# Scattering the last row's expert lists between the gathers of the first expert blocks, in a decoder layer on one core

## The chip, the cores and the metric

The kernel runs on one core of a Trainium2 chip. The metric is the device time of one execution in microseconds; lower is better. Engines: PE (TensorE), DVE (VectorE), ACT (ScalarE), POOL (GpSimd) and SP (SyncE, which only issues DMAs here).

## The reference

One decoder layer over x (4 rows of 512 tokens, 512 wide): attention, then a state-space scan that takes a context, then a mixture of experts. The change lies in the start of the last of these:

```python
logits = x @ gate_weight.T                      # 2048 tokens, 32 experts
topv, topi = top_k(softmax(logits), 8)
active = scaled >= 0.05                         # at least the best one stays
for e in experts:                               # w_gu: 512 -> 384, w_d: 192 -> 512
    g, u = split(x @ w_gu[e].T)
    acc = acc + (silu(g) * u) @ w_d[e].T * combine[:, e]
return x + acc
```

## The kernel before

The four rows pass through attention and scan one after the other. At the end of each row DVE works out, for each of its 512 tokens, the routing weights (`entry`, 33 numbers: 32 weights and the token's number) and up to eight places (`slot[:, t, k]`), one in the list of each expert that the token is active for. MAX8 puts them in the order of the experts: place k = 0 belongs to the token's lowest expert, so the list of expert e is filled by the scatters of k = 0 to e and by none of a higher k. POOL writes the lists into DRAM by indirect DMAs (`send`, line 2039), one for each t (4 tiles of 128 tokens) and k (8): 32 scatters a row. Those of the first three rows count on one semaphore, `sent`; those of the last row on eight, `sent0` to `sent7`, one for each k (`send_last`).

After the last row DVE counts the lists and writes a table of blocks (`tab`, `blocks`, lines 1947 to 1974; `rows_ok` says it is there). A block is 128 entries of one expert's list; each expert has at least two (`MIN_BLK`), and here there are 68 in all. A quad is four blocks. Each block passes through these steps:

- SP (`load_quad`) loads the block's weights (`meta`, line 469) and its token numbers (`get_ids`, line 470), and the numbers once more for the add (`add_ids`, line 473). For the first 16 blocks (`early`), block b first waits until `sent` of k = b // 2 has landed.
- POOL gathers the 128 token rows (`get`, line 2072) into one of four buffers `x_blk`, once `get_ids` is there (`get_in`) and PE has transposed the buffer's last block (`xt_ps`). `get_next(q, r)` gathers the block that lies six behind q * 4 + r.
- PE transposes the block (line 519), ACT and DVE split it in a high and a low part (`xt_hi`, line 1396; `xt_lo`, line 1979), PE multiplies by the expert's gate and up weights (lines 917 to 919), ACT and DVE make the hidden activations, PE transposes them and multiplies by the down weights (lines 932 to 936), and ACT weighs the result into one of four `y_ring` buffers (line 1409).
- POOL adds the block into `out` by an indirect DMA that accumulates (`add`, line 2078). `add_pair` waits for y, for `add_ids`, and for earlier adds to have landed.

PE's order is written out by hand: gate_up of block b + 1, the transposes of block b + 3, down of block b, the transposes of b + 1's hidden activations. So a gather that is late holds up the down product of the block three ahead of it. POOL executes its DMAs in the order of the program; so does SP. The expert weights are loaded by ACT's queue, four experts ahead.

The lines of SP that make a block wait for its scatters, and POOL's order before the change:

```python
if early and r % MIN_BLK == 0:
    sp.wait_ge(S[f"sent{(q * QUAD + r) // MIN_BLK}"], TT * 16)
```

```
k0 k1 k2 k3 k4 | gathers 0 1 2 3 | gathers 4 5 | k5 gathers 6 7 adds 0 1 | k6 gathers 8 9 adds 2 3 | k7 gathers 10 11 adds 4 5 | gathers 12 13 adds 6 7 | ...
```

Of the kernel before, what the change touches and what calls it, by code (L numbers as in the profile page):

```python
# [35 lines left out]
NE, INTER, TOPK, TAU = 32, 192, 8, 0.05  # L36
# [5 lines left out]
QUAD = 4  # L42
# [97 lines left out]
def decoder_layer(nc, a):  # L140
    ctx = ExitStack()
    with ctx:
# [38 lines left out]
        def sb(name, shape, dt=F32):  # L181
# [74 lines left out]
        r = {n: o_t[:].rearrange("p h t -> p (h t)")[:, 12 * T + i * TT * NE:12 * T + (i + 1) * TT * NE].rearrange("p (t e) -> p t e", t=TT)  # L256
             for i, n in enumerate(NAMES)}
# [52 lines left out]
        def wait_apart(eng, semaphore, value):  # L310


            if isinstance(value, int):
                eng.wait_ge(semaphore, value)
                return
            count = eng.to_reg(value)
            eng.wait_ge(S["w_in_sb"], 16 * N_W)
            eng.wait_ge(semaphore, count)
# [1710 lines left out]
        def _(pool):  # L2029
# [7 lines left out]
            def send(t, k, sent):  # L2037

                pool.indirect_dma_start(out=lists, out_offset=bass.IndirectOffsetOnAxis(ap=slot[:, t, k:k + 1].bitcast(U32), axis=0),  # L2039
                                        in_=entry[:, t, :], in_offset=None, bounds_check=LIST_ROWS - 1, oob_is_err=False).then_inc(sent, 16)  # L2040
# [23 lines left out]
            def send_last(ks):  # L2064

                for k in ks:
                    for t in range(TT):
                        send(t, k, S[f"sent{k}"])

            def get(r):  # L2070

                pool.indirect_dma_start(out=x_blk[:, r, :], out_offset=None, in_=xf_dram,
                                        in_offset=bass.IndirectOffsetOnAxis(ap=get_ids[:, r:r + 1].bitcast(U32), axis=0),
                                        bounds_check=NTOK - 1, oob_is_err=False).then_inc(S[f"blk_in{r}"], 16)

            def add(r):

                pool.indirect_dma_start(out=out, out_offset=bass.IndirectOffsetOnAxis(ap=add_ids[:, r:r + 1].bitcast(U32), axis=0),  # L2078
                                        in_=y_ring[:, r, :], in_offset=None, compute_op=ALU.add).then_inc(S[f"added{r % 2}"], 16)

            def get_next(q, r):

                far = r + QUAD + 2
                fq, fr = far // QUAD, far % QUAD
                wait_apart(pool, S[f"get_in{fr}"], q * 32 + (fq * 32 + 32))
                wait_apart(pool, S["xt_ps"], q * QUAD + (far - QUAD + 1))
                get(fr)

            def landed_before(q, r):
                return pool.value_load(blocks[0:1, bass.ds(q * QUAD + (B_LANDED + r), 1)], min_val=ADDED0 - 16, max_val=ADDED0 + MAX_BLK * 8)  # L2090

            def add_pair(q, r):

                landed = [landed_before(q, r), landed_before(q, r + 1)]
                for i in range(2):
                    wait_apart(pool, S[f"add_in{r + i}"], q * 16 + 16)
                for i in range(2):
                    wait_apart(pool, S["yb_ok"], q * QUAD + (r + i + 1))
                    wait_apart(pool, S[f"added{i}"], q * 32 + (ADDED0 + (r // 2) * 16))
                    wait_apart(pool, S[f"added{1 - i}"], landed[i])  # L2100
                    add(r + i)

            pool.wait_ge(S["slot_ok"], NB)

            send_last(range(0, 5))
            pool.wait_ge(S["xf_out"], NB * 16)
            pool.wait_ge(S["blank_ok"], 1)
            pool.wait_ge(S["rows_ok"], 2)
            for r in range(QUAD):
                pool.wait_ge(S[f"get_in{r}"], 32)  # L2110
                get(r)
            last_quad = pool.value_load(tab[0:1, T_LAST:T_LAST + 1], min_val=NE * MIN_BLK // QUAD - 1, max_val=MAX_BLK // QUAD - 1)
            pool.wait_ge(S["x2_out"], NB * 16)
            for r in range(2):
                get_next(-1, r + 2)
            for q in range(2):
                for r in range(0, QUAD, 2):
                    k = q * 2 + r // 2 + 5
                    if k < TOPK:
                        send_last(range(k, k + 1))  # L2120
                    get_next(q, r)
                    get_next(q, r + 1)
                    add_pair(q, r)
            with pool.Fori(2, last_quad) as q:
                for r in range(0, QUAD, 2):
                    get_next(q, r)
                    get_next(q, r + 1)
                    add_pair(q, r)
# [47 lines left out]
```

## Time and profile before

| | us |
|---|---|
| median of three runs | 1611.66 |
| lowest, highest | 1605.77, 1620.83 |
| the profiled execution | 1605.77 |
| its span, first to last instruction | 1604.0 |
| last row's scatters begin | 1228.78 |
| first gather of the expert phase | 1254.52 |
| mean granted TensorE clock | 0.947 of full speed |

All times in the rows are microseconds from the start of the profiled execution's span. The span ends with the expert phase, so what this phase starts later or loses is in the time in full, unless a later stretch has slack. A timeline's row gives the start, the duration, the engine, the line, what is written and read, and in brackets how long the engine had been idle and what ended that. SPq is SP's own queue; the row of a DMA there is its issue. The chain of waits follows the end of the program back to its start, from each instruction to what released it.

### The profile page before, as it was taken

The page shows a single profiled execution, that of the slowest core. Times are in us where ns is not written, and L with a number is a line of the kernel's source. Part 1 is how long each engine was busy: PE and PEld are TensorE (multiplying, and loading weights), DVE is VectorE, ACT ScalarE, POOL GpSimd, SP SyncE. Part 2 cuts the span into 40 slices and gives each one's busy share as a digit, 9 for nine tenths or more (in the row PEclk, how much of TensorE's full clock was granted, in tenths as well). Part 3 has the DMA queues.
Part 4 walks back from the last instruction along what each step waited for, and adds up shares of the span by engine and source line. Part 5 has one row for each costly group of instructions (what it writes and reads, how often), then busy time and mean ns, then how long its engine had stood idle before and what let it go on. Part 6 is the DMA issues. An engine that isn't in the chain of part 4 may idle for free.

```text
span 1604.0 us, 25043 instructions
## 1 busy us (share of the span) xinstructions
PE 1391.2 (87%) x6762; PEld 993.4 (62%) x6763; DVE 1222.9 (76%) x1459; ACT 972.1 (61%) x2484; POOL 472.7 (29%) x307
## 2 busy tenths in 40 slices
PE   4799889999999899989999998998943489999996
PEld 1577666547777554667765366776422367777775
DVE  4477768959898996889899688899986156776763
ACT  6677665477876546787654578866420246666663
POOL 0000000000000781000068300004842576655663
PEclk9799999999999999999999899999975689999998
DMA  6693333222253221235313232520701379999994
GB/s 241 239 287 101 90 105 93 66 65 83 78 171 106 87 76 42 93 92 158 93 61 116 55 92 80 142 69 29 239 32 39 66 167 239 252 240 245 244 212 64
DMA packets 128788, 202.45 MB, mean 126 GB/s; under 512 B 44984, under 2 KB 46473, under 8 KB 127552
## 3 DMA queue, kind: packets, MB, share of 16 engines
q1 hardware_dynamic: 75120, 86.70, 18.7%
q0 software_dynamic: 27840, 63.83, 16.9%
q10 hardware_dynamic: 25744, 50.87, 9.9%
q8 instruction: 44, 0.72, 0.2%
q14 instruction: 40, 0.33, 0.1%
HBM read 170.57 MB, written 46.21 MB: 135 GB/s over the span
## 4 chain that ended last, share of the span: by engine, by line
PE 40%; DVE 34%; ACT 11%; issue 7%; DMA 2%; ACTq 2%; another core or an unknown queue 1%; POOL 1%; SPq 1%; DVEq 0%; POOLq 0%
DVE state L1581 12%; PE pair_o L661 6%; DVE dbu L1573 5%; DVE dbu L1587 5%; DVE y L1592 4%; PE bank L643 4%; PE bank L797 4%; PE pair_o L797 3%; PE bank L917 2%; PE pair L595 2%; PE pair L597 2%; PE pair L596 2%; ACT decay L1117 2%; PE pair L519 2%; PE bank L918 2%
## 5 line engine op out<-in xcount | busy, mean ns | idle before, releaser
L2039 POOL DMA_INDIRECT lists<-entry,slot x128 | 253.9, 1983 | 207.6 <-DVE slot L1764 169.8
L1581 DVE TENSOR_TENSOR_SCAN state<-decay,dbu 128x2048 f32<-128x2048 f32 x64 | 283.0, 4422 | 7.5 <-ACT decay L1117 4.0
L661 PE MATMUL pair_o<-v_aug,probs 128*128 128x129 f32 x2048 | 250.7, 281 | 8.9 <-ACT probs L1111 8.6
L2035 POOL DMA_DIRECT2D wq<-wq_dram x30 | 21.5, 719 | 783.6 <-PE pair L597 670.0
L661 PEld LDWEIGHTS pair_o<-v_aug,probs 128*128 128x128 f32 x2048 | 241.2, 196 | 17.7 <-ACT probs L1111 16.8
L1117 ACT ACTIVATE decay<-delta,neg_a 128x511 f32<-128x511 f32 x256 | 165.0, 738 | 100.4 <-DVE state L1581 93.7
L1111 ACT ACTIVATE probs<-bank 128x512 f32<-128x512 f32 x256 | 146.5, 606 | 88.1 <-PE bank L643 51.2
L2078 POOL DMA_INDIRECT out<-y_ring,add_ids x68 | 118.4, 1742 | 101.3 <-DMA out<-y_ring,add_ids 70.7
L1587 DVE TENSOR_TENSOR dbu<-state,c_bc 128x2048 f32<-128x2048 f32 x64 | 146.6, 2291 | 1.6
L1573 DVE TENSOR_TENSOR dbu<-du,b_bc 128x2048 f32<-128x2048 f32 x64 | 146.3, 2287 | 1.6
L1592 DVE TENSOR_TENSOR y<-y,dbu 128x2048 f32<-128x2048 f32 x60 | 137.2, 2287 | 1.1
L643 PE MATMUL bank<-q_t,k_t 128*128 128x512 f32 x256 | 122.7, 614 | 12.0 <-ACT q_t L1099 6.8
L797 PE MATMUL bank<-wout,o_t 128*128 128x512 f32 x256 | 125.0, 620 | 0.9 <-DMA wout<-in_wout 0.9
L797 PE MATMUL pair_o<-wout,o_t 128*128 128x512 f32 x256 | 120.3, 600 | 0.0
L595 PE MATMUL pair<-wq,xn_hi 128*128 128x512 f32 x256 | 106.7, 417 | 4.4 <-ACT q_s L1082 3.5
L917 PE MATMUL bank<-w_hi,xt_hi 128*128 x272 | 100.1, 368 | 8.0 <-DVE xt_lo L1979 6.9
L597 PE MATMUL pair<-wq,xn_lo 128*128 128x512 f32 x256 | 100.7, 393 | 0.0
L596 PE MATMUL pair<-wq,xn_hi 128*128 128x512 f32 x256 | 100.6, 393 | 0.0
L1632 DVE TENSOR_TENSOR w_lo<-w_raw,w_hi (+1 forms) x64 | 95.4, 1494 | 1.9
L918 PE MATMUL bank<-w_lo,xt_hi 128*128 x272 | 93.9, 345 | 0.0
L919 PE MATMUL bank<-w_hi,xt_lo 128*128 x272 | 93.8, 345 | 0.0
L1071 ACT ACTIVATE junk<-pair 128x128 bf16<-128x128 f32 x256 | 67.3, 291 | 39.0 <-PE pair L597 39.0
(239 smaller groups left out, 2690.3 us busy)
## 6 DMA issues: line engine op xcount, KB each, us to landing
wq<-wq_dram POOLq DMA_DIRECT2D x30, 1024.0 KB, 8.5
w_raw<-in_w_exp ACTq DMA_DIRECT2D x32, 768.0 KB
wout<-in_wout SPq DMA_DIRECT2D x64, 256.0 KB
b_bc<-bc_dram SPq DMA_DIRECT2D x64, 256.0 KB
c_bc<-bc_dram SPq DMA_DIRECT2D x64, 256.0 KB
w_raw<-in_w_exp ACTq DMA_DIRECT2D x32, 512.0 KB
lists<-in_const ACTq DMA_DIRECT2D x1, 8712.0 KB, 49.3
q_s<-in_x SPq DMA_DIRECT2D x4, 1024.0 KB, 5.1
```

Of the source, the lines that this page charges most:

```text
L595: pe.matmul(bank_q[t % 2][:], xn_hi[:, k, tile], wq[:, 0, k, :], start=(k == 0), stop=False)
L597: mm = pe.matmul(bank_q[t % 2][:], xn_lo[:, k, tile], wq[:, 0, k, :], start=False, stop=(k == KT - 1))
L643: mm = pe.matmul(bank_s[k % 2][:], k_t[:, tile], q_t[:, j, :], start=True, stop=True)
L661: mm = pe.matmul(bank_o[half][:, (t % 2) * (DH + 1):(t % 2 + 1) * (DH + 1)], probs[:, k, t * P:(t + 1) * P], v_aug[:, k, :], start=(k == 0 ...
L797: mm = pe.matmul((bank_o + bank_s)[t][:], o_t[:, h, t * P:(t + 1) * P], wout[:, h % 4, :], start=(h == 0), stop=(h == H - 1))
L1111: act.activation(probs[:, k, :], bank_s[k % 2][:], ACT.Exp).then_inc(S["exp_ok"], 1)
L1117: act.activation(dA3[:, e, 1:], delta[:, e, 1:], ACT.Exp, scale=neg_a[:, bass.ds(n, 1), e:e + 1].rearrange("p a c -> p (a c)")).then_inc(S ...
L1573: dve.tensor_tensor(dbu[:], du[:], b_bc[:, i:i + 1, :].to_broadcast([P, ET, T]), ALU.mult).then_inc(S["dbu_ok"], 1)
L1581: dve.tensor_tensor_scan(state[:].rearrange("p e t -> p (e t)"), dA, dbu[:].rearrange("p e t -> p (e t)"), 0.0, ALU.mult, ALU.add).then_in ...
L1587: dve.tensor_tensor(dbu[:], state[:], c_bc[:, i:i + 1, :].to_broadcast([P, ET, T]), ALU.mult).then_inc(S["bc_free"], 1)
L1592: dve.tensor_tensor(dst[:], y[:], dbu[:], ALU.add).then_inc(S["y_ok"], 1)
L2039: pool.indirect_dma_start(out=lists, out_offset=bass.IndirectOffsetOnAxis(ap=slot[:, t, k:k + 1].bitcast(U32), axis=0), in_=entry[:, t, :] ...
```

## The change

POOL issues the last row's scatters in another order. k0 and k1 stay ahead of the gathers. k2 now lies between the gathers of blocks 1 and 2, k3 behind the gather of block 3, and k4 to k7 each directly ahead of a pair of gathers (before, k5 to k7 stood ahead of pairs of gathers two slots earlier). The order is then:

```
k0 k1 | gathers 0 1 | k2 | gathers 2 3 | k3 | gathers 4 5 | gathers 6 7 adds 0 1 | k4 gathers 8 9 adds 2 3 | k5 gathers 10 11 adds 4 5 | k6 gathers 12 13 adds 6 7 | k7 gathers 14 15 adds 8 9 | ...
```

SP, PE, ACT and DVE are as before. The loads, gathers and adds are the same ones.

```diff
-            send_last(range(0, 5))
+            send_last(range(0, 2))
             pool.wait_ge(S["xf_out"], NB * 16)
             pool.wait_ge(S["blank_ok"], 1)
             pool.wait_ge(S["rows_ok"], 2)
-            for r in range(QUAD):
+            for r in range(2):
                 pool.wait_ge(S[f"get_in{r}"], 32)
                 get(r)
+            send_last(range(2, 3))
+            for r in range(2, QUAD):
+                pool.wait_ge(S[f"get_in{r}"], 32)
+                get(r)
+            send_last(range(3, 4))
+            for r in range(2):
+                get_next(-1, r + 2)
             last_quad = pool.value_load(tab[0:1, T_LAST:T_LAST + 1], min_val=NE * MIN_BLK // QUAD - 1, max_val=MAX_BLK // QUAD - 1)
             pool.wait_ge(S["x2_out"], NB * 16)
-            for r in range(2):
-                get_next(-1, r + 2)
             for q in range(2):
                 for r in range(0, QUAD, 2):
-                    k = q * 2 + r // 2 + 5
-                    if k < TOPK:
+                    k = q * 2 + r // 2 + 3
+                    if k in range(4, TOPK):
                         send_last(range(k, k + 1))
                     get_next(q, r)
                     get_next(q, r + 1)
                     add_pair(q, r)
+            send_last(range(TOPK - 1, TOPK))
             with pool.Fori(2, last_quad) as q:
```

## Rows read from the trace of the kernel before

**Rows 1.** Table of stretches: length, busy time (instructions) by engine, PEclk, DMA share, GB/s.

```profile
1206.00:1258.00 52.00, 14.04 (x73) 11.38 (x74) 23.38 (x85) 2.70 (x5) 21.72 (x22) 0.53 0.11 30
1258.00:1325.00 67.00, 51.71 (x237) 42.26 (x238) 28.25 (x57) 27.48 (x48) 42.12 (x34) 0.85 0.61 137
1325.00:1560.00 235.00, 227.16 (x1180) 182.32 (x1179) 163.04 (x307) 153.39 (x257) 144.29 (x102) 1.00 0.98 242
```

**Rows 2.** Chain of waits, 1180 to 1604 us: start, length, what it is.

```profile
1254.52 3.25 DMA x_blk<-xf_dram,get_ids
...
1272.51 8.45 another core or an unknown queue
...
1290.13 2.26 another core or an unknown queue
...
1308.97 3.37 another core or an unknown queue
```

**Rows 3.** Timeline of POOL: scatters (L2039), gathers (L2072) and adds (L2078).

```profile
1237.80 0.98 POOL L2039 DMA_INDIRECT lists<-entry,slot  x1 [0.30 <-issue]
...
1253.23 0.98 POOL L2039 DMA_INDIRECT lists<-entry,slot  x1 [0.30 <-issue]
1254.52 1.05 POOL L2072 DMA_INDIRECT x_blk<-xf_dram,get_ids  x1 [0.30 <-issue]
...
1262.98 1.00 POOL L2072 DMA_INDIRECT x_blk<-xf_dram,get_ids  x1 [5.27 <-DMA get_ids<-lists]
...
1275.81 1.05 POOL L2072 DMA_INDIRECT x_blk<-xf_dram,get_ids  x1 [0.31 <-issue]
1277.17 1.02 POOL L2072 DMA_INDIRECT x_blk<-xf_dram,get_ids  x1 [0.30 <-issue]
...
1305.67 0.98 POOL L2039 DMA_INDIRECT lists<-entry,slot  x1 [0.30 <-issue]
...
1309.64 1.63 POOL L2078 DMA_INDIRECT out<-y_ring,add_ids  x1 [0.30 <-issue]
...
1313.46 1.08 POOL L2072 DMA_INDIRECT x_blk<-xf_dram,get_ids  x1 [0.30 <-issue]
...
1323.49 1.08 POOL L2072 DMA_INDIRECT x_blk<-xf_dram,get_ids  x1 [0.30 <-issue]
```

**Rows 4.** Timeline of SP's queue: issues of the block loads.

```profile
1247.87 0.02 SPq L470 DMA_DIRECT2D get_ids<-lists  x1
...
1256.33 0.70 SPq L470 DMA_DIRECT2D get_ids<-lists  x1
...
1259.95 0.35 SPq L469 DMA_DIRECT2D meta<-lists  x1
...
1262.04 0.35 SPq L469 DMA_DIRECT2D meta<-lists  x1
...
1310.86 0.69 SPq L469 DMA_DIRECT2D meta<-lists  x1
```

**Rows 5.** Timeline of DVE: the last write of the block table.

```profile
1239.36 0.40 DVE L1974 CAST blocks<-bank 1x256 int32<-1x256 f32 x1
```

**Rows 6.** Timeline of ACT: blocks 0 and 14 taken up (xt_hi), y of block 0.

```profile
1259.05 0.60 ACT L1396 ACTIVATE xt_hi<-pair 128x512 fp32r<-128x512 f32 x1 [43.01 <-PE pair L519]
...
1271.55 0.69 ACT L1409 ACTIVATE y_ring<-pair_o,meta 128x512 f32 x1 [0.97 <-issue]
...
1336.32 0.60 ACT L1396 ACTIVATE xt_hi<-pair  x1 [0.17 <-issue]
```

**Rows 7.** Timeline of PE: one gate_up product after the 8 us gap, one later.

```profile
1282.72 0.52 PE L918 MATMUL bank<-w_lo,xt_hi 128*128 x1
...
1288.18 0.34 PE L918 MATMUL bank<-w_lo,xt_hi 128*128 x1
```

**Rows 8.** Line 2039 in 1050 to 1200 us and 1200 to 1320 us: duration ns min/median/max.

```profile
L2039 POOL DMA_INDIRECT lists<-entry,slot x32: 980/2022/4162, 1101.6 to 1182.8; - x32
...
L2039 POOL DMA_INDIRECT lists<-entry,slot x32: 980/982/1748, 1228.8 to 1305.7; - x32
```

## The prediction

> **What bounds the kernel now.** I read four views in this order. First the table of stretches: from 1325 to 1560 us PE is busy for 227.16 of 235 us at a granted clock of 1.00, so the expert phase, once it runs, is limited by TensorE and can't catch up what it lost earlier. Before it lie two poor stretches: 1206 to 1258 us (PE busy 14.04 of 52) and 1258 to 1325 us (51.71 of 67, clock 0.85) [rows 1]. These two are all that the change touches. Then the chain of waits: it enters the expert phase through the scatters of the lists, then the gather of block 0 (issued at 1254.52, landed 3.25 us later), then PE's first transposes. Behind that it names pieces of 8.45, 2.26 and 3.37 us that no recorded work explains [rows 2]. Then POOL's timeline: the eighth of the last row's 32 scatters starts at 1237.80 and the twentieth at 1253.23, a pitch of 1.286 us; the gather of block 0 waits behind all twenty [rows 3]. Last SP's queue, which loads the token ids that each gather needs [rows 4].
>
> **The change part by part.** No instruction is added or removed. What moves is where POOL issues scatters. Before: k0 to k4, gathers 0 to 5, then k5, k6 and k7 each ahead of a pair of gathers. After: k0, k1, gathers 0 and 1, k2, gathers 2 and 3, k3, gathers 4 to 7, adds 0 and 1, then k4, k5, k6 and k7, each directly ahead of its own pair of gathers and adds. The wait for x2_out moves too, behind gathers 4 and 5. SP issues that store ahead of xf's, and xf_out is waited for ahead of gather 0 already, so I cost it at nothing; were x2 late, add 0 and gather 6 would wait, in both kernels.
>
> What matters is a wait that isn't in the diff: SP loads the ids of blocks 2k and 2k+1 only when the scatters of slot k have landed (the early part of load_quad). Before, k5 stood ahead of the gathers of blocks 6 and 7, which need k3: two slots of slack. After, k4 stands ahead of blocks 8 and 9, which need k4 itself: no slack, four times over.
>
> *The head start.* The blocks' table is ready at 1239.36 + 0.40 = 1239.76 [rows 5]; eight scatters end at 1237.80 + 1.29 = 1239.09, so neither waits for the other. Then SP must load the ids of block 0. From a load of meta to the gather is 1262.98 - 1259.95 = 3.03 us [rows 3, 4]. At the earliest gather 0 starts at 1239.76 + 3.03 = 1242.8. At the latest SP is as slow as before, get_ids at 1247.87, and the gather 3.03 later, 1250.9. Nothing says which, so I take the middle, 1246.9. That is 7.6 us ahead of 1254.52.
>
> *POOL's order from there.* SP's pitch from one block to the next is 1262.04 - 1259.95 = 2.09 us [rows 4]; a gather takes 1277.17 - 1275.81 = 1.36 of POOL, two adds 1313.46 - 1309.64 = 3.82, four scatters 4 x 1.286 = 5.14 [rows 3]. Gather 1 at 1249.0, k2 from 1250.4 to 1255.5, gathers 2 and 3 to 1258.2, k3 with its last scatter at 1262.1 and over at 1263.4, gathers 4 and 5 to 1266.1. Gather 6 must wait for the ids that depend on k3.
>
> *The price of that wait,* W, from the start of the last scatter of a slot to the gather of its first block. Upper end: the last scatter of k7 starts at 1305.67 and SP's load of meta for block 14 at 1310.86, 5.19 us, though that load also waited for a free buffer; plus 3.03 for meta to gather, 8.2. Lower end: the scatter's own 0.98 and the 3.03, 4.0, with a landing that costs nothing more. No row shows the landing alone; I take the middle, W = 6.1.
>
> The Trainium skill bears on this (DMA: Bandwidth & Descriptors, section Anatomy of one DMA, SWDGE path): it gives a DMA issued by GpSimd a fixed cost of about 2.0 us whatever its size, most of it the receipt of the last write before the semaphore moves. By that page W would be about 2.0 + 3.0, some 5 us, which is the point from which the first rival decides, and the sum below would be about 0; the 3.25 us of the gather above, which also moves data, doesn't contradict it.
>
> So gather 6 is at 1262.1 + 6.1 = 1268.2, gather 7 at 1270.3, add 0 at 1271.6; y of block 0 is ready by then (17.0 us after its gather, as 1271.55 - 1254.52 [rows 3, 6], is 1263.9). Adds end at 1275.5. From here each slot costs POOL three scatter pitches 3.86 + W 6.1 + 2.09 for the second gather + 1.36 + 3.82 = 17.2 us. Gather 14 comes after k4, k5, k6 and then k7: 1275.5 + 3 x 17.2 + 3.86 + 6.1 = 1337.1, against 1323.49 before.
>
> *What of it is on the path.* Before, ACT takes up block 14 at 1336.32, and gather 0 was picked up 1259.05 - 1254.52 = 4.53 us after its issue [rows 3, 6]; so gather 14 was needed only by 1331.8. After, it is 5.3 us late, PE has waited for it, and behind it there are 54 blocks at PE's own pace. POOL catches up at once (two gathers and two adds are 6.5 us a pair), so the lateness stays 5.3 and doesn't grow. Waiting also lowers PE's clock: a gate_up matmul takes 0.52 us after the 8 us gap and 0.34 later [rows 7]; twelve of them are 2.2 us, and I add one such block. Sum: 5.3 + 2.2 = +7.5 us. The profiled execution took 1605.77 us, which is the fastest of three with a median of 1611.66; the sum gives 1613.3 against the first and 1619.2 against the median, which is what I predict.
>
> **The rivals.**
>
> *The head start stays.* If W is near its lower end (4.0), the slot costs 15.1 us and gather 14 is at 1337.1 - 5 x 2.1 = 1326.6 (k3's W and four more), before 1331.8. It is 5.2 us early, and PE, which started 7.6 earlier, keeps that much: 1611.7 - 5.2 = 1606.5. With gather 0 at 1242.8 rather than 1246.9 PE keeps the 7.6: 1604. It decides at W = 5.0, where 5 x 1.1 takes the whole lateness away. For it: before, gather 14 is issued 8.3 us ahead of its need (1331.8 - 1323.49), so POOL wasn't what PE waited for. Against: no row of a scatter shows its data landed as soon as issued.
>
> *PE's unexplained pieces come with the scatters.* The 8.45, 2.26 and 3.37 us of the chain begin at 1272.51, 1290.13 and 1308.97 [rows 2]: the first just ahead of gather 6 at 1275.81, where POOL issues k5, the last 3.3 us behind k7's last scatter at 1305.67, and three scatter batches run beside PE. After the change six batches do. Three more at the mean of 4.7 are 14.1 us; if they delay y and with it POOL's adds, they come on top: 1619.2 + 14.1 = 1633.3. Against it: when PE waits for POOL anyway, such a piece is hidden, and POOL's pauses between scatters and gathers may even end them.
>
> *SP stays slow.* Its get_ids for block 0 is at 1247.87 and for block 1 at 1256.33, 8.5 us instead of 2.09, while POOL scatters [rows 4]. If that comes back in only two of the slots, 2 x 6.4 = 12.8 us more: 1632.
>
> *Scatters take longer beside VectorE.* In the stretch of VectorE's long scans 32 scatters had a median of 2022 ns, up to 4162; in the last batch it is 982, up to 1748 [rows 8]. If the 16 scatters of k4 to k7 cost 1.04 us more each, that is 16.6: 1636. The Trainium skill has the reason (SBUF, State Buffer, section Who interferes with whom: a VectorE instruction in a two-port mode holds the port pair that it shares with GpSimd, and GpSimd is blocked until it ends). The trace shows slow scatters in the scans' stretch only, and doesn't show by itself that the port is why.
>
> **How the numbers follow.** Forecast 0.50, with its own range 1611 (no lateness is left) to 1630 (W at 8.2, 5 x 2.1 = 10.5 more); head start 0.15; pieces with the scatters 0.15; slow SP 0.13; slow scatters 0.05. The range of all, 1604 to 1636, reaches from the first rival to the last and leaves the lateness of an SP slow in all slots outside. A measurement of this kernel tells about 1% from no change, 16 us, so faster means below 1595.5 and slower above 1627.8. Even the head start alone doesn't reach the first: 0.05 for faster, for a W at its end together with pieces that vanish. Slower takes nearly all of the last three rivals, less where they overlap with hidden waits: 0.29. Within 1%: 0.66.
>
> **What would show it.** Right: gather 0 at about 1247, PE's first transposes about 7 us earlier; POOL idle for 3 to 5 us between each of k4 to k7 and the gather behind it, ended by get_ids; gather 14 at about 1337; PE waiting for x_blk in 1280 to 1340; from 1345 the same pace as before. Wrong: POOL not idle behind the scatters (head start), more pieces of unexplained time while x_blk has landed (second rival), SP's loads 8 us apart (third), scatters over 2 us (fourth). The forecast falls altogether if gather 14 starts before 1331.8 and the time still rises.

## The result: 2.6% slower, and half of it is lost after the change's own stretch

| | us |
|---|---|
| after, median of 4 (lowest, highest) | 1654.3 (1649.44, 1667.81) |
| before, median of 4 in the same comparison | 1612.55 (1605.77, 1620.83) |
| ratio, 95% interval | 1.0257 [1.0211, 1.0304] |
| the profiled execution's span | 1652.1, before 1604.0 |
| mean granted TensorE clock in it | 0.929, before 0.947 |

The prediction was 1619.2 us, within 1604 to 1636. The kernel is outside of it, on the slow side. All ratios in this document compare fast executions alone, while the medians have the slow ones in them too (here the one of 1667.81 us, in e10 two of twelve, and in one comparison a single 4568.49 us of the kernel before).

To compare traces I count from T0, the start of the first of the last row's 32 scatters. T0 itself isn't the change's: it lies behind the same instructions in all kernels, and over all profiles here it is at 1221.9 to 1240.0 us. In the two main profiles it is 1228.8 (before) and 1237.7 (after), so 9.0 of the 48.1 us between the spans lie ahead of anything that was changed. The other 39.1 us are the subject. Each number of this table is one row's time less T0:

| us after T0 | before | after | later by |
|---|---|---|---|
| gather of block 0 | 25.7 | 15.1 | -10.6 |
| add of block 0 | 49.7 | 40.4 | -9.3 |
| gather of block 14 | 94.7 | 120.1 | 25.4 |
| y of block 14 | 123.2 | 143.2 | 20.0 |
| y of block 67, the last | 364.7 | 398.9 | 34.2 |
| end | 375.2 | 414.4 | 39.1 |

20.0 us are lost up to y of block 14, and another 14.2 between there and the last block, where the two programs are the same. The remaining 4.9 fall in the tail behind it. These are the numbers of one profiled execution each; the last experiments give second and third profiles.

The table of stretches of after, with the columns of [rows 1] (length, then busy time and instructions of PE, PEld, DVE, ACT, POOL, then PEclk, DMA share, GB/s):

```profile
1206.00:1258.00 52.00, 17.75 (x76) 14.70 (x76) 28.84 (x99) 3.91 (x10) 11.55 (x12) 0.50 0.17 55
1258.00:1325.00 67.00, 45.50 (x214) 37.30 (x215) 25.52 (x52) 25.00 (x45) 36.74 (x32) 0.82 0.46 110
1325.00:1560.00 235.00, 197.79 (x987) 154.91 (x986) 138.61 (x258) 127.85 (x214) 144.45 (x95) 0.95 0.85 207
```

The stretches are counted from the start of the span, in which T0 of after lies 9.0 us later. Against [rows 1], PE is busy 3.7 us more in the first stretch (the head start), 6.2 less in the second, and 29.4 less in the third, which the prediction took to be PE's own.

POOL's timeline of after shows the head start and the waits behind the late scatters:

```profile
1246.74 0.98 POOL L2039 DMA_INDIRECT lists<-entry,slot  x1 [0.30 <-issue]
1252.83 1.04 POOL L2072 DMA_INDIRECT x_blk<-xf_dram,get_ids  x1 [5.11 <-DMA get_ids<-lists]
...
1309.82 1.90 POOL L2039 DMA_INDIRECT lists<-entry,slot  x1 [0.30 <-issue]
1316.63 1.05 POOL L2072 DMA_INDIRECT x_blk<-xf_dram,get_ids  x1 [4.91 <-DMA get_ids<-lists]
1319.26 1.01 POOL L2072 DMA_INDIRECT x_blk<-xf_dram,get_ids  x1 [1.58 <-DMA get_ids<-lists]
1321.11 1.63 POOL L2078 DMA_INDIRECT out<-y_ring,add_ids  x1 [0.83 <-DMA add_ids<-lists]
1323.04 1.58 POOL L2078 DMA_INDIRECT out<-y_ring,add_ids  x1 [0.31 <-issue]
1324.92 1.04 POOL L2039 DMA_INDIRECT lists<-entry,slot  x1 [0.30 <-issue]
...
1349.77 0.98 POOL L2039 DMA_INDIRECT lists<-entry,slot  x1 [0.30 <-issue]
1357.85 1.05 POOL L2072 DMA_INDIRECT x_blk<-xf_dram,get_ids  x1 [7.09 <-issue]
```

and SP's queue beside it, the loads that follow the last scatters of slots k5 and k7:

```profile
1313.69 0.35 SPq L469 DMA_DIRECT2D meta<-lists  x1
...
1354.76 0.35 SPq L469 DMA_DIRECT2D meta<-lists  x1
```

Gather 0 is at 1252.83 instead of 1254.52 although T0 is 9.0 us later. Then each slot stands still: from the last scatter of k5 (1309.82) SP takes 3.87 us to its next load and 2.94 more to the gather; behind k7 (1349.77) it is 4.99 and 3.09. The row at 1357.85 is the gather of block 14. What PE did meanwhile is in the waits of 1258 to 1400 us (engine and line, what it waited for, total us, times, longest):

```profile
PE pair L519 <- DMA x_blk<-xf_dram,get_ids: 43.0, 8, 10.7
...
POOL x_blk L2072 <- DMA get_ids<-lists: 22.5, 5, 7.4
```

PE waits 43.0 us for gathered blocks. That is the predicted mechanism, and it is larger than predicted. The second loss is in the waits of 1400 to 1560 us, past all scatters. Before:

```profile
POOL out L2078 <- DMA out<-y_ring,add_ids: 42.8, 18, 3.2
ACT y_ring L1409 <- PE pair_o L936: 25.8, 27, 1.0
```

After:

```profile
ACT y_ring L1409 <- PE pair_o L936: 42.5, 33, 2.4
...
POOL out L2078 <- DMA out<-y_ring,add_ids: 27.8, 11, 3.7
...
PEld pair_o L932 <- issue: 9.0, 13, 1.4
...
PE pair_o L932 <- DMA out<-y_ring,add_ids: 2.0, 2, 1.1
```

In both kernels POOL's add waits for an earlier add to land, 42.8 and 27.8 us. What is new is that PE's down product (line 932), which has no row at all in this view of before, now waits as well: a y_ring buffer is free only when the add four blocks back has landed, and PE waits for that (`added`) ahead of `down`. The view puts only 2.0 us of it down to the adds by name; the 9.0 us of the weight load it calls "issue", which names no releaser. The chain of waits for the same 160 us is plainer; these are its shares by line, cut at the end. Before:

```profile
by line: issue 20.9%; PE bank L917 11.8%; PE bank L918 9.7%; PE bank L919 9.6%; PE pair L519 6.1%; ACT xt_hi L1396 4.8%; PE pair_o L936 4.1%; PE bank L519 3.8%; ACTq L1302 3.7%; PE pair_o L932 2.4%; PE pair_o L935 2.2%; DVE xt_lo L1979 2.2%
```

After:

```profile
by line: DMA out<-y_ring,add_ids 37.7%; issue 13.2%; DMA x_blk<-xf_dram,get_ids 8.1%; DMA get_ids<-lists 5.1%; PE bank L917 3.2%; DMA add_ids<-lists 3.1%; PE bank L919 2.6%; PE bank L918 2.6%; PE pair L519 2.5%; PE pair_o L936 1.9%; PE pair
```

Before, the adds aren't in the chain and PE's products are. After, the landing of adds is its largest part. The same view of the other profiles divides them in the same way: the landing of adds has 63 to 75% in e1 to e5, e8, e10 and e11, none in e9a, 6.3% in e9b (the kernel before both times), and none in e6 and e7, whose adds are shorter. Two questions follow: how much each half of the change costs, and whether the slower pace is a lasting effect of a single late gather.

### The profile page after: what moved, and what is told of

It is laid out like the page before. It is cut to its first block, busy times and chain, and to the rows that moved or that the text cites. A ratio compares the mean times of both kernels' runs of the same rounds, so it can differ in the third digit from the quotient of the medians.

```text
span 1652.1 us, 25043 instructions
## 1 busy us (share of the span) xinstructions
PE 1415.5 (86%) x6762; PEld 1009.3 (61%) x6763; DVE 1223.9 (74%) x1459; ACT 970.9 (59%) x2484; POOL 490.0 (30%) x307
## 4 chain that ended last, share of the span: by engine, by line
PE 38%; DVE 28%; DMA 11%; ACT 10%; issue 7%; SPq 2%; POOL 2%; ACTq 1%; POOLq 1%; DVEq 0%
DVE state L1581 10%; PE pair_o L661 8%; DMA out<-y_ring,add_ids 7%; PE bank L643 5%; DVE dbu L1573 5%; DVE y L1592 4%; DVE dbu L1587 4%; PE bank L797 4%; PE pair_o L797 3%; PE pair L595 2%; PE pair L597 2%; PE pair L596 2%; ACT decay L1117 2%; ACT probs L1111 2%; PE bank L519 1%
## 5 line engine op out<-in xcount | busy, mean ns | idle before, releaser
L2039 POOL DMA_INDIRECT lists<-entry,slot x128 | 254.4, 1987 | 213.1 <-DVE slot L1764 175.4
L661 PE MATMUL pair_o<-v_aug,probs 128*128 128x129 f32 x2048 | 256.9, 286 | 8.6 <-ACT probs L1111 8.3
L661 PEld LDWEIGHTS pair_o<-v_aug,probs 128*128 128x128 f32 x2048 | 247.5, 200 | 17.4 <-ACT probs L1111 16.5
L1111 ACT ACTIVATE probs<-bank 128x512 f32<-128x512 f32 x256 | 146.3, 605 | 98.5 <-PE bank L643 52.1
L2078 POOL DMA_INDIRECT out<-y_ring,add_ids x68 | 126.8, 1865 | 94.2 <-DMA out<-y_ring,add_ids 44.0
L1979 DVE TENSOR_TENSOR xt_lo<-pair,xt_hi (+1 forms) x70 | 48.3, 690 | 81.2 <-ACT xt_hi L1396 79.9
L2072 POOL DMA_INDIRECT x_blk<-xf_dram,get_ids x70 | 83.9, 1198 | 60.3 <-DMA get_ids<-lists 28.4
L1396 ACT ACTIVATE xt_hi<-pair (+1 forms) x70 | 41.9, 598 | 100.0 <-PE pair L519 97.7
L1409 ACT ACTIVATE y_ring<-pair_o,meta 128x512 f32 x68 | 46.8, 688 | 85.1 <-PE pair_o L936 85.1
```

Source lines behind the costliest of these rows:

```text
L661: mm = pe.matmul(bank_o[half][:, (t % 2) * (DH + 1):(t % 2 + 1) * (DH + 1)], probs[:, k, t * P:(t + 1) * P], v_aug[:, k, :], start=(k == 0 ...
L1111: act.activation(probs[:, k, :], bank_s[k % 2][:], ACT.Exp).then_inc(S["exp_ok"], 1)
```

## The experiments

In all of them "pace" is the time for a pair of blocks, from ACT's y rows: (y of 34 - y of 14) / 10, then (y of 58 - y of 34) / 12. "Behind y" is the mean time from a block's y to the start of its add, even and odd blocks, over blocks 16 to 57.

| | median | g14 | y14 | end | pace | behind y |
|---|---|---|---|---|---|---|
| before | 1612.55 | 94.7 | 123.2 | 375.2 | 9.20, 9.20 | 3.9, 1.7 |
| after | 1654.3 | 120.1 | 143.2 | 414.4 | 10.13, 9.62 | 10.3, 7.8 |
| e1 early start, two slots of slack | 1618.07 | 97.5 | 123.7 | 388.0 | 9.47, 9.60 | 9.5, 7.0 |
| e2 early start, one slot | 1619.41 | 92.0 | 118.5 | 379.7 | 9.55, 9.38 | 9.2, 6.8 |
| e3 late half alone | 1646.6 | 120.1 | 143.4 | 413.5 | 10.15, 9.46 | 10.1, 7.6 |
| e4 after, adds first | 1638.76 | 121.4 | 144.3 | 407.0 | 9.47, 9.56 | 9.3, 6.9 |
| e5 before, one hold-up | 1620.37 | 107.5 | 129.1 | 390.6 | 9.44, 9.49 | 9.3, 6.9 |
| e6 after, half-width adds | 1628.34 | 119.7 | 141.6 | 391.1 | 9.20, 9.19 | 7.5, 5.2 |
| e7 before, half-width adds | 1592.55 | 90.1 | 116.8 | 366.7 | 9.20, 9.20 | 2.2, 1.6 |
| e8 before, only k7 late | 1616.88 | 97.6 | 122.2 | 390.3 | 10.07, 9.49 | 10.0, 7.5 |

g14 (gather of block 14), y14 and end are us after T0 in the one profiled execution; the median is over several. They differ: where a reading rests on the one or the other, the text says which. One profile is a coarse measure of the end: two profiles of one program differ there by 10.0 us (e2 and e10, see below) and by 25.0 (after and e11). The kernel before has medians of 1612 to 1615 in the comparisons, so a ratio is given for each.

**The two halves of the change.** e1 keeps the early start (k0 and k1 ahead of the first gathers) and gives k5 to k7 the two slots of slack that they had before. The cuts of e1, e3, e4 and e10 are against after, those of e5, e7 and e8 against before:

```diff
             for r in range(2):
                 get_next(-1, r + 2)
+            send_last(range(4, 5))
...
-                    k = q * 2 + r // 2 + 3
-                    if k in range(4, TOPK):
+                    k = q * 2 + r // 2 + 5
+                    if k in range(5, TOPK):
                         send_last(range(k, k + 1))
...
-            send_last(range(TOPK - 1, TOPK))
```

> The early half of the change alone: k0 and k1, gathers 0 and 1, k2, gathers 2 and 3, k3, gathers 4 and 5, k4, then k5, k6 and k7 ahead of pairs of gathers as before, each two slots ahead of the blocks that need it. Theory A (the four waits without slack cost the time): no gather behind gather 6 waits for its ids, POOL's slots take 12 to 17 us as before, and the earlier start gives 3 to 10 us: 1603 to 1610. Rival (the early interleaving itself costs, for instance because scatters slow PE's start): slower than before, 1618 or more.

e2 is the same with one slot of slack: `k = q * 2 + r // 2 + 4` in the loop, k4 in its first round, and nothing behind it.

> The early half, with one slot of slack: k4 ahead of gathers 6 and 7, k5 ahead of 8 and 9, and so on to k7 ahead of 12 and 13. Theory A: a slot of POOL without a wait is 12 to 14 us and the scatters' landing and the ids together take 8, so one slot hides it whole: within 3 us of the kernel with two slots, 1603 to 1612. Rival (each slot taken away costs in proportion): half way to the changed kernel, about 1630.

e3 keeps only the late half: k0 to k3 ahead of all gathers, and k4 to k7 each directly ahead of its own blocks, as in after.

```diff
-            send_last(range(0, 2))
+            send_last(range(0, 4))
...
-            for r in range(2):
-                pool.wait_ge(S[f"get_in{r}"], 32)
-                get(r)
-            send_last(range(2, 3))
-            for r in range(2, QUAD):
+            for r in range(QUAD):
                 pool.wait_ge(S[f"get_in{r}"], 32)
                 get(r)
-            send_last(range(3, 4))
```

> The late half alone: k0 to k3, then gathers 0 to 7 and adds 0 and 1, then k4 to k7 each directly ahead of its own gathers as in the changed kernel. Theory A: four waits of 7 to 8 us stay, slots of 20 to 21 us, so the time is that of the changed kernel within 6 us, 1648 to 1660. Rival (early interleaving costs): near the kernel before, 1612 to 1620.

Measured: e1 1618.07 us, ratio 1.0015 [0.9972, 1.0058]; e2 1619.41, 1.0033 [0.9976, 1.0090]; e3 1646.6, 1.0189 [1.0152, 1.0226]. The late half alone costs 31.7 us (against a median of 1614.9 for the kernel before in that comparison), of the change's 41.7, and its gather 14 and y of block 14 are where those of after are (120.1 and 143.4). The early start alone brings nothing that the times can tell: e1 is at the time of its rival and not in the 1603 to 1610 expected, e2 between its two theories, and e3 1.4 us below its range. In its profiles it is real at first: gather 0 is at 15.1 instead of 25.7, and in e2 y of block 14 comes 4.7 us earlier than before. By the end that is gone, and both end later than before does from T0. Two things in the profiles stand against it. The first is a kind of wait that [rows 2] show too. The waits of e1 from 1250 to 1345 us have

```profile
ACT silu_g L1401 <- remote: 16.8, 2, 15.1
ACT xt_hi L1396 <- remote: 4.1, 3, 2.8
```

where the same view of before has

```profile
ACT silu_g L1401 <- remote: 10.7, 2, 8.5
```

"remote" means that no recorded work explains the wait. ACT waits for a PE product whose record ended long ago. The second is the pace behind block 14: 9.4 to 9.6 us a pair instead of 9.20, with gathers that were in time. So the pace isn't tied to a late gather 14, and I tested it by itself.

**One suspected cost alone.** e8 is the kernel before with k7 alone moved to directly ahead of its blocks:

```diff
-                    if k < TOPK:
+                    if k < TOPK - 1:
                         send_last(range(k, k + 1))
...
+            send_last(range(TOPK - 1, TOPK))
             with pool.Fori(2, last_quad) as q:
```

> The kernel before with k7 alone moved, from ahead of gathers 10 and 11 to directly ahead of gathers 14 and 15: one slot without slack. POOL waits 7 to 8 us once. Theory X: gather 14 had 8.3 us in hand, nothing is lost, 1609 to 1615. Theory L: the adds are late by the wait less the 2 to 4 us that they have in hand, 4 to 6 us lost, 1616 to 1619.

Measured: 1616.88 us (median of ten), 1.0033 [0.9997, 1.0069]. The wait is there, in POOL's timeline of e8:

```profile
1319.52 0.98 POOL L2039 DMA_INDIRECT lists<-entry,slot  x1 [0.30 <-issue]
1326.44 1.76 POOL L2072 DMA_INDIRECT x_blk<-xf_dram,get_ids  x1 [5.94 <-issue]
```

6.92 us for W, and gather 14 is at 97.6, inside the 103.0 by which the prediction said it was needed; y of block 14 comes at 122.2, 1.0 us ahead of before. It is late all the same. PE's timeline of e8 has, at the transposes of block 14:

```profile
1330.73 1.09 PE L519 MATMUL pair<-const,x_blk 128*128 128x128 f32 x4 [4.82 <-DMA x_blk<-xf_dram,get_ids]
```

The 103.0 comes from a profile in which PE was held back by the unexplained pieces of [rows 2]. e5 to e8 have none. In e5, which is the kernel before up to its hold-up, y of block 10 is at 98.6, and in e7 at 98.5, against 104.8 in the profile of before; in e8 it is at 95.0. From y of block 10 to y of block 12 e8 then takes 16.7 us, where before takes 9.4. So a gather is needed by a moment that moves with PE, and y14 of e5 and e8 is better held against the 116.8 of e7 than against 123.2. The larger part of the loss comes behind it: from T0 to the end the profile is 15.1 us longer than that of before (390.3 against 375.2), and from y of block 14 to the end it takes 268.1 us against 252.0, at a pace of 10.07 and then 9.49. In this execution, a POOL that was held up for 7 us never got back to where it was. The medians tell a smaller loss, 4.8 us, whose interval reaches no loss at all.

**A hold-up without any scatter.** e5 leaves the scatters where they were before and puts eight memsets of a spare tile on POOL, one after the other, ahead of the loop:

```diff
+            for i in range(8):
+                pool.memset(spare[:], 0.0).then_inc(S["idle"], 1)
+                pool.wait_ge(S["idle"], i + 1)
             with pool.Fori(2, last_quad) as q:
```

> The kernel before with POOL held up once, by eight memsets of an unused tile of 128x2048 directly ahead of gather 14, D us in all (some 15 to 25). The scatters keep their order. Theory X (only a late gather costs, and POOL catches up): gather 14 had 8.3 us in hand, so D - 8 us are lost and the pace of a pair of blocks behind it is 9.2 us as before. Theory L (POOL's adds wait for the last pair to land, so that POOL's own cycle is as long as PE's and it never catches up): D - 4 or more are lost, adds follow y by 8 to 10 us instead of 2 to 4 to the end, and the pace behind is 9.5 us or more.

Measured: 1620.37 us (median of ten, 1615.05 to 1632.32), 1.0054 [1.0034, 1.0074]. The profile shown is of its slowest execution. The spare tile and the semaphore `idle` are declared elsewhere. POOL's timeline:

```profile
1329.80 1.58 POOL L2079 DMA_INDIRECT out<-y_ring,add_ids  x1 [0.31 <-issue]
1330.82 15.45 POOL L2126 MEMSET spare<- 128x2048 f32 x8
1347.46 1.09 POOL L2073 DMA_INDIRECT x_blk<-xf_dram,get_ids  x1 [1.20 <-issue]
...
1378.49 1.63 POOL L2079 DMA_INDIRECT out<-y_ring,add_ids  x1 [1.03 <-issue]
1380.42 2.90 POOL L2079 DMA_INDIRECT out<-y_ring,add_ids  x1 [0.31 <-issue]
...
1387.54 1.63 POOL L2079 DMA_INDIRECT out<-y_ring,add_ids  x1 [0.97 <-DMA out<-y_ring,add_ids]
1389.47 2.97 POOL L2079 DMA_INDIRECT out<-y_ring,add_ids  x1 [0.31 <-issue]
...
1396.86 1.63 POOL L2079 DMA_INDIRECT out<-y_ring,add_ids  x1 [1.23 <-DMA out<-y_ring,add_ids]
```

The memsets put gather 14 12.8 us later than before; y of block 14 is 5.9 late, and the end 15.4. (Against e7, the nearer measure up to block 14, gather 14 is 17.4 late and y of block 14 12.3 late.) The even add of one pair starts at 1378.49, the next at 1387.54 and 1396.86, 9.05 and 9.32 apart, and each waits for the last pair's odd add: 1396.86 - 1389.47 = 7.39 us from the start of one to the start of the other. Over blocks 15 to 57 these are 7.53 on average, and 1.93 from the even to the odd add of a pair. That is a cycle of 9.46 us on average, longer than the 9.20 in which PE delivers a pair. The chain of e5 for 1400 to 1560 us:

```profile
by line: DMA out<-y_ring,add_ids 71.7%; issue 17.6%; POOL out L2079 6.4%; POOLq L319 1.3%; DMA get_ids<-lists 1.2%; POOLq L317 0.5%; POOLq L2128 0.5%; POOLq L318 0.4%; SPq L470 0.3%; SPq L466 0.3%; POOLq L2073 0.3%; SPq L474 0.3%; SPq L471 
```

So the expert phase can run at two paces. At the pace of before, PE sets it and the adds follow y by 3.9 and 1.7 us. At the other, the adds follow by 9.3 and 6.9 us, and the chain of adds sets it. One hold-up is enough to go from the first to the second, and behind block 14 no profile shows the way back. Ahead of it there is one: in the three profiles of before the add of block 4 is 9.8 to 9.9 us behind its y and that of block 8 only 1.7 to 3.1, while PE itself takes 11.5 to 13.8 us for a pair. The adds catch up where PE is slower than they are.

The size in the medians doesn't speak for this theory as the profile does. The memsets take 15.45 us. Theory L expected a loss of that less 4 or more, at least 11.5 us; theory X, that less 8, 7.5 us. The medians differ by 8.3.

**Shorter adds.** e6 is after and e7 is before with adds of half the width (`y_ring[:, r, 0:D // 2]` into a DRAM tensor `half` of 256 columns). Both leave out the experts' part of the output, so their times stand only against each other. Width and target change together, so which of the two shortens an add isn't separated.

```diff
-                pool.indirect_dma_start(out=out, out_offset=bass.IndirectOffsetOnAxis(ap=add_ids[:, r:r + 1].bitcast(U32), axis=0),
-                                        in_=y_ring[:, r, :], in_offset=None, compute_op=ALU.add).then_inc(S[f"added{r % 2}"], 16)
+                pool.indirect_dma_start(out=half, out_offset=bass.IndirectOffsetOnAxis(ap=add_ids[:, r:r + 1].bitcast(U32), axis=0),
+                                        in_=y_ring[:, r, 0:D // 2], in_offset=None, compute_op=ALU.add).then_inc(S[f"added{r % 2}"], 16)
```

> The changed kernel with half adds: only columns 0 to 255 of y are added, into a DRAM tensor of its own, so the experts' part of the output is left out. Against the kernel before with the same half adds. Theory L: the adds land sooner, POOL's cycle is shorter than PE's, POOL catches up and the pace is 9.2 us from about block 16; the difference to the kernel before with half adds is the slots' alone, 20 to 28 us instead of 42. Theory X: the adds have no part in it, the difference stays about 42 us.

> The kernel before with the same half adds, the experts' part of the output left out. All theories: PE is the bound, so within 6 us of the kernel before, 1600 to 1612.

Measured: e6 1628.34 us, e7 1592.55; against the kernel before 1.0083 [1.0050, 1.0115] and 0.9881 [0.9850, 0.9912]. The chain of e6 for 1400 to 1560 us:

```profile
by line: issue 21.7%; PE bank L918 9.8%; PE bank L920 7.4%; PE bank L919 7.4%; ACT xt_hi L1397 6.8%; ACTq L1303 5.5%; PE pair_o L937 4.7%; PE pair L520 4.6%; ACT silu_g L1402 3.4%; ACTq L1410 2.9%; PE pair_o L933 2.6%; PE pair_o L936 2.5%; 
```

The adds are out of the chain and PE is back in it, at a pace of 9.20 and 9.19 with the adds still 7.5 and 5.2 us behind y. The one add to the next pair's takes 7.16 + 1.97 = 9.13 us, just under PE's 9.20. From y of block 14 to that of 67 the two profiles take 241.6 and 241.3 us: the second loss has vanished, and with it nothing else, since y of block 14 is still 24.8 us late. From T0 to the end they differ by 24.4, the two profiled executions by 28.5, of which 4.0 is T0 (1239.8 and 1235.8). The medians differ by 35.8, which lies between what the two theories gave, and only 5.9 below the 41.7 of the full adds. By the ratios it is 32.6 against 41.4, with intervals that overlap. The pace is settled by the profiles, the size in the medians isn't. e7 missed its own range too: it was expected at 1600 to 1612, since PE bounds it, and is 19.6 us below the kernel before. In its profile PE's pace is the same 9.20, and from T0 to the end it is 8.5 us shorter, 6.4 of that up to y of block 14; the rest of the 19.6 is open.

**Can the wait lie beside the adds?** e4 is after with `add_pair(q, r)` ahead of the two `get_next` of each slot, so that POOL adds while SP waits for the scatters.

```diff
                         send_last(range(k, k + 1))
+                    add_pair(q, r)
                     get_next(q, r)
                     get_next(q, r + 1)
-                    add_pair(q, r)
```

> The changed kernel with one difference: in the four unrolled slots the two adds stand between the scatters and the gathers, so POOL has 3.8 us of work while the ids come. Theory A: each of three or four slots is 3.8 us shorter (about 17 us), and the time falls by 11 to 15 us from 1654, to about 1640. Rival (the length of the slots isn't what counts): unchanged at 1650 to 1658.

Measured: 1638.76 us, 1.0138 [1.0096, 1.0179], so the median is 15.5 us below that of after. The trace doesn't bear out the reason. Gather 14 is at 121.4, no earlier than in after, and POOL's timeline has

```profile
1321.65 0.98 POOL L2039 DMA_INDIRECT lists<-entry,slot  x1 [0.30 <-issue]
1333.44 1.59 POOL L2078 DMA_INDIRECT out<-y_ring,add_ids  x1 [10.81 <-issue]
1335.33 1.58 POOL L2078 DMA_INDIRECT out<-y_ring,add_ids  x1 [0.30 <-issue]
1337.21 1.08 POOL L2072 DMA_INDIRECT x_blk<-xf_dram,get_ids  x1 [0.30 <-issue]
```

The adds don't use the wait, they have it themselves: SP loads `add_ids` of a block behind `get_ids` of the block six further on, which it must not load before the scatters have landed. SP's queue in e4 shows it:

```profile
1325.05 0.33 SPq L470 DMA_DIRECT2D get_ids<-lists  x1
1326.15 0.33 SPq L473 DMA_DIRECT2D add_ids<-lists  x1
...
1328.96 0.33 SPq L473 DMA_DIRECT2D add_ids<-lists  x1
```

From T0 to the end e4 is 7.4 us shorter than after, 6.6 of it by the pace from block 14 to 34 (9.47 instead of 10.13), which is less than two profiles of one kernel differ by. I had the right time for the wrong reason, and why e4 is faster stays open.

**Can the adds be kept close?** e10 was written as e2 with another order in the slots, the adds ahead of the next scatters and gathers:

```diff
+            send_last(range(4, 5))
+            get_next(0, 0)
+            get_next(0, 1)
+            for s in range(4):
+                add_pair(s // 2, s % 2 * 2)
+                if s < 3:
+                    send_last(range(s + 5, s + 6))
+                    get_next((s + 1) // 2, (s + 1) % 2 * 2)
+                    get_next((s + 1) // 2, (s + 1) % 2 * 2 + 1)
```

> An attempt to beat both: the early start and one slot of slack, and in the unrolled slots the adds ahead of the scatters and gathers, so that adds stay close behind y. Order: k0 k1, gathers 0 1, k2, gathers 2 3, k3, gathers 4 5, k4, gathers 6 7, adds 0 1, k5, gathers 8 9, adds 2 3, k6, gathers 10 11, adds 4 5, k7, gathers 12 13, adds 6 7, then the loop. Theory L: adds 2 to 5 us behind y, pace 9.2, and 3 to 8 us faster than before, 1604 to 1609. Rival: the order of adds in the first slots doesn't last, adds 7 to 9 us behind y and 1612 to 1619 as for the kernel with one slot of slack.

Measured: 1624.32 us (12 runs), 1.0050 [1.0013, 1.0087]; in its profile gather 14 is at 94.0, y of block 14 at 123.2, the end at 389.7, the adds 9.4 and 7.0 us behind y, the pace 9.53 and 9.70. The question isn't answered by it. Written out, its order is k4, gathers 6 and 7, adds 0 and 1, k5, gathers 8 and 9, adds 2 and 3, and so on to k7, gathers 12 and 13, adds 6 and 7, and that is e2's: the 170 indirect DMAs of POOL from T0 on stand in the same sequence in both traces. So e10 is a second profile of e2's program and twelve more executions of it, and its median of 1624.32 against 1619.41 shows how far two samples of one program lie apart. In it the adds of blocks 4 and 6 start 14.9 and 17.7 us behind their y, and POOL is idle only 0.30 us ahead of each: they wait for nothing of their own but for what stands before them in POOL's order. From there on they stay late. No complete kernel here beats the one before.

**The same kernels again.** e9a and e9b are the kernel before and e11 is after, unchanged, for a second and third profile.

> The kernel before once more, for a second profile. Theory L: adds follow y by 2 to 4 us and a pair of blocks takes 9.20 us behind block 14, as in the first profile. Rival (the first profile, the fastest of its runs, was an exception): adds 7 to 9 us behind y and a pace of 9.4 to 9.6 us here too.

> The kernel before, a third profile. As for the second; beside it, the unexplained pieces in PE (8.45, 2.26 and 3.37 us in the first profile): theory L expects nothing of them; if they belong to the scatters beside PE they stand in each profile of this kernel, if they are chance they are missing in some.

> The changed kernel once more, for a second profile. Theory A with L: from the first of the last 32 scatters, gather 14 at 116 to 124 us, y of block 14 at 140 to 147 us, and behind it a pace of 9.5 to 10.2 us for a pair.

Measured: 1611.52, 1597.66 and 1670.0 us, one execution each. Both of before run at 9.20 and 9.19 to 9.20 a pair with the adds 3.8 to 4.0 and 1.7 to 1.8 behind y, end at 373.8 and 374.0 after T0 (375.2 in the first), and have waits that nothing explains, of 1 to 4 us. T0 is at 1235.9 and 1221.9: the 14 us between these two executions are all ahead of the stretch. e11 has gather 14 at 125.4 and runs at 10.63 and 10.65 a pair, slower again than the first profile of after, with the adds 12.8 and 10.5 behind y; it ends at 439.4. All three numbers of e11 lie above what was expected of it (gather 14 at 116 to 124, y of block 14 at 140 to 147, it came at 148.8, a pace of 9.5 to 10.2). So the faster of the two paces is what all three profiles of before have, and neither of after; and the slow one has no single value. One thing stands beside its values: in e11 the even add of a pair takes over 2 us on POOL in 20 of the 22 pairs from block 14 to 57, and the odd one starts 2.8 to 2.9 us behind it; in the stretch with a pace of 10.1 the even add is that long in 4 of 10 pairs in the first profile of after and in e8, and in 2 in e3, and in none of the 12 pairs behind it, where the pace is 9.5 to 9.6.

## Why the prediction was wrong, step by step

**The head start: right, and a little better.** Gather 0 was forecast at 18.1 us after T0 (1246.9 - 1228.8), and came at 15.1. The early end of the range, 1242.8, would be 14.0. SP was not slow once POOL stopped scattering. Add 0, forecast at 42.8, came at 40.4.

**The wait that isn't in the diff: right in kind.** POOL idles behind k4 to k7, the releaser is get_ids (the profile names it in three of the four slots), and gather 14 carries the sum.

**W: mis-sized.** The forecast took 6.1 us, the middle of 4.0 to 8.2. The four slots have 8.38, 6.81, 7.90 and 8.08, mean 7.8. The part that no row of before showed alone, from the start of a slot's last scatter to SP's next load, is 2.87, 3.87, 5.04 and 4.99 us. The upper bound, the one pair of rows in which a scatter and SP's load followed each other (k7 and block 14, [rows 3, 4]), was the better estimate. I took it down because of a free-buffer wait that could have explained it, and had no measurement of that. The Trainium skill (DMA: Bandwidth & Descriptors, section Anatomy of one DMA, SWDGE path) gives such a DMA about 2.0 us of fixed cost, from which the prediction estimated a W of some 5: all four slots lie above that.

**The rest of the slot: mis-sized.** 2.09 us for the second gather was SP's pitch in the first quad, where a block's three loads follow one another. From block 10 on the `add_ids` load is for another block (`add_tokens` reads the table again and checks for a landed add), and SP's pitch is 2.7; the second gather came 1.36, 2.63, 2.72 and 2.70 us behind the first. A third term was left out: in the slot of k4 the add of block 3 waits 3.89 us for its y, because PE is itself waiting for gathers. Together a slot took 22.5, 19.1, 20.6 and 21.2 us instead of 17.2. So gather 14 was at 120.1 after T0 instead of 108.3, and late by 17.1 us instead of 5.3. y of block 14 is 20.0 late; the 2.9 between them aren't taken apart (the 2.2 forecast for the clock would be most of it; the granted clock in 1258 to 1325 us is 0.82 against 0.85). e3 shows that the late half does it alone.

**"POOL catches up at once": wrong.** This is the step that failed. With the slots mis-sized as above but POOL catching up, the sum would have been 1611.7 + 20.0 = 1631.7, inside the range; what came behind y of block 14 took it out. I took POOL's need for a pair to be its busy time, 6.5 us, against PE's 9.2. But each pair of adds waits for the landing of the last pair, and POOL can't do the next adds meanwhile. The cycle of before is 7.07 us from the odd add to the next even one, which waits for its landing, and 2.13 to the odd one: 9.20. Only the second has any room (1.93 when nothing but POOL sets it), so the chain needs about 9.0 us (the two cycles from block 4 to block 8, in which the adds of before catch up, take 8.1 to 9.4). The page of the kernel before hinted at it, with 101.3 us of idle time ahead of the adds, 70.7 of it ended by an add's landing:

```profile
L2078 POOL DMA_INDIRECT out<-y_ring,add_ids x68 | 118.4, 1742 | 101.3 <-DMA out<-y_ring,add_ids 70.7
```

What I took for a reserve was the latency of a chain. Delayed, this chain takes 7.53 + 1.93 = 9.46 us a pair (e5), more than PE. So the delay isn't repaid but passed on, through y_ring, to PE. That is shown from three sides, by the profiles: e5 (it is there behind a hold-up with no scatter moved), e8 (it is there behind a single slot without slack, which costs PE one wait of 4.8 us), e6 (with shorter adds it doesn't happen, after a hold-up as large as that of after). Its size is 14.2 us in the profile of after.

**The sum.** Against +7.5 us forecast the profiles show 39.1: 20.0 for the slots, 14.2 for the adds' pace, 4.9 in the tail, where the last adds have also to land. The medians show 41.7.

**The rivals.** *The head start stays*: no, W is above the 5.0 where it decides. e2 shows that it wouldn't pay even with slack. *PE's unexplained pieces come with the scatters*: the first profile of after, with six batches beside PE, has none, and all three of before do; they aren't tied to how many scatters lie beside PE. *SP stays slow*: no, its loads of meta for the two blocks of a slot are 1.6 to 2.7 us apart. *Scatters take longer*: 0.98 to 1.90 us in the slots, most of them under 1.1: no. (For the slow scatters of the scans' stretch, the VectorE instructions beside them are TENSOR_TENSOR of 2.29 us and TENSOR_TENSOR_SCAN of 4.42 us; no run here shows that they are in the two-port mode that the prediction gave as the reason.) The rival that came true, a hold-up that persists because adds form a chain as long as PE's, wasn't among them.

**Left open.** Why the landings are 0.4 us longer (7.5 against 7.07) once the adds are late, and what makes the even adds of e11 long. Why e1 and e2 (e10 too) go to the slow pace and before doesn't, although PE waits for no gather in them behind 76 us after T0; what differs is that the add of block 8 is 7.8 and 9.2 us behind its y in e1 and e2, and 1.7 to 3.1 in before. The three profiles of before all have unexplained pieces that slow PE while the adds catch up, and no profile shows this kernel with full adds and without such pieces; so whether e5 and e8 went to the slow pace by their hold-up alone, and whether all unprofiled executions of before run at 9.20, isn't shown. What the unexplained pieces are: ACT waits for products of PE whose records have ended 2 to 17 us before. They show, as waits that no recorded work ends, in all three profiles of before, in e1, e2, e4 and e10, with single waits of 2 to 4 us in e3 and e11, and not in the first profile of after nor in e5 to e8. And why T0 moves over 18 us in code that is the same.

## What to carry to other kernels

An engine's reserve is not its idle time. Where its instructions wait for the landing of their own forerunners, take the whole cycle (start of one to start of the next, with the wait) and put it against the bound's pace: here 9.0 to 9.5 against 9.2 us a pair, next to no reserve, where the busy time said 6.5. The moment by which something is needed, too, is read from one profile, and moves when that profile has lost time of its own: here by 6 us. Two kernels that read differently can be one program, as e2 and e10 are: write out each engine's order before reading a difference between them. When an edit takes slack away, look for what is queued behind the wait on other engines too (SP's load for the adds stood behind its load for the gathers), and price an unseen latency by the nearest row that contains it rather than by the middle to zero.

## What the runs showed of the hardware

- An indirect scatter of 128 rows by POOL, then a load on SP's queue that waits for it: 2.87 to 5.04 us from the start of the one to the issue of the other, of which 0.98 to 1.90 is the scatter's own time on POOL (four slots of after; 3.85 in e8).
- An accumulating indirect DMA of 128 rows of 2 KB: the next one that waits for its landing starts 7.0 to 7.1 us after it on average in the three profiles of before, and 7.5 to 7.6 in those at the slow pace. With 1 KB rows it is 7.16 us in e6, whose adds are late, and 5.56 in e7, whose adds also wait for y: so it can be shorter than 7, and half the bytes don't halve it.
- An add takes 1.6 us on POOL, but some take longer at either pace: from block 16 to 57, 6 to 9 of the 21 odd adds take 2.0 to 2.6 us in the profiles of before, and 8 to 12 of them mostly 2.9 to 3.0 where the adds are late (1380.42 and 1389.47 in e5 above). In e11 and e7 it is the even one instead, and in e6 none.
- Three executions of the kernel before differ by 14 us in when the last row's scatters begin, and all profiles here, the same programs up to there, by 18, without any disturbance that shows in these views.
